# Gate weights for all experts in one GpSimd product, their sum and the row places on ScalarE

## The reference

```python
h = tok_embedding(x)                                  # position, nesting and segment tables times W
h = h + attn(layernorm(h))                            # 8 heads, kernelised attention in chunks of 128
h = h + ffn(layernorm(h))

def ffn(x):                                           # the part that the change touches
    gates = softmax(x @ Wg + bg)
    vals, idx = top_k(gates, 2)
    vals = vals / (sum(vals) + 0.01)
    w = sum(one_hot(idx, 8) * vals)                   # weight of each expert for each token, 0 for six of them
    y = relu(x @ W1[e] + b1[e]) @ W2[e] + b2[e]       # for each expert e
    return sum over e of w[e] * y[e]
```

## Time and profile before

| | |
|---|---|
| median of the runs | 360.71 us |
| profiled execution | 361.17 us |
| its span, first to last instruction | 359.4 us |
| mean granted TensorE clock | 0.981 |
| TensorE busy | 336.3 us, 94% |
| VectorE busy | 309.7 us, 86% |
| ScalarE busy | 251.1 us, 70% |
| GpSimd busy | 210.9 us, 59% |

### The profile page before, as it was taken

The page is one execution under the profiler, slowest core; times in us unless marked ns, Lnnn a source line. Parts: engine busy times, 40 slices in busy tenths (PEclk is TensorE's granted clock), DMA queues, the critical chain, the costliest instruction groups (busy, mean ns, idle before and its releaser), DMA issues.

```text
span 359.4 us, 11506 instructions
## 1 busy us (share of the span) xinstructions
PE 336.3 (94%) x3017; PEld 293.4 (82%) x3017; DVE 309.7 (86%) x1214; ACT 251.1 (70%) x665; POOL 210.9 (59%) x413
## 2 busy tenths in 40 slices
PE   7959999999999999999998799999999999999982
PEld 2525788888878887878886699999999999999982
DVE  6778899999988999999999687998997777678986
ACT  1644878988877987877976477676776677667730
POOL 7010311677777677777776877887875455545520
PEclk9985999999999999999999999999999999999998
DMA  6066660000110001000010312232333322226859
GB/s 165 19 181 168 208 219 3 11 25 35 36 36 25 12 35 34 33 25 17 24 35 34 86 44 80 81 89 87 106 112 90 88 76 64 78 80 190 247 143 275
DMA packets 33131, 30.46 MB, mean 85 GB/s; under 512 B 4701, under 2 KB 27320, under 8 KB 33080
## 3 DMA queue, kind: packets, MB, share of 16 engines
q1 hardware_dynamic: 25848, 18.81, 18.5%
q0 software_dynamic: 4224, 9.18, 7.6%
q10 hardware_dynamic: 3008, 1.89, 1.8%
HBM read 16.42 MB, written 13.44 MB: 83 GB/s over the span
## 4 chain that ended last, share of the span: by engine, by line
PE 80%; DVE 8%; issue 4%; DMA 2%; ACT 2%; SPq 1%; POOL 0%; DVEq 0%; ACTq 0%; POOLq 0%
PE ps_oy L1826 9%; PE ps_vc L1826 9%; PE ps_out L1816 8%; PE ps_out L1719 8%; PE ps_oy L1736 7%; PE ps_q L1816 7%; PE ps_vc L1709 5%; PE ps_qT L1701 3%; PE ps_oy L1729 3%; PE ps_k L1667 2%; PE ps_qT L1808 2%; PE ps_k L1816 2%; PE ps_vc L1690 2%; PE ps_vc L1692 2%; PE ps_vc L1691 2%
## 5 line engine op out<-in xcount | busy, mean ns | idle before, releaser
L773 POOL DMA_INDIRECT y_dram<-heads_out,place x68 | 68.8, 1011 | 46.5 <-ACT heads_out L950 36.8
L750 POOL DMA_INDIRECT slots_dram<-rows,row_id x64 | 64.5, 1007 | 18.4 <-issue 17.6
L941 ACT ACTIVATE k_prime<-ps_out,b_T 128x128 f32<-128x128 f32 x105 | 31.0, 365 | 19.3 <-PE ps_out L1816 18.6
L941 ACT ACTIVATE k_prime<-ps_q,b_T 128x128 f32<-128x128 f32 x108 | 31.7, 365 | 17.2 <-PE ps_q L1816 17.0
L1826 PE MATMUL ps_oy<-w_tile,k_prime 128*128 128x128 f32 x288 | 38.6, 277 | 1.2 <-issue 1.2
L1826 PE MATMUL ps_vc<-w_tile,k_prime 128*128 128x128 f32 x280 | 37.4, 277 | 0.8 <-issue 0.6
L1816 PE MATMUL ps_out<-sT,w_tile 128*128 128x128 f32 x280 | 37.0, 275 | 0.0
L1719 PE MATMUL ps_out<-context,qT 128*128 128x130 f32 x256 | 36.9, 288 | 0.0
L1826 PEld LDWEIGHTS ps_oy<-w_tile,k_prime 128*128 128x128 f32 x288 | 35.0, 192 | 2.0 <-issue 1.9
L715 POOL TENSOR_TENSOR rstd<-moments,ln_eps 128x4 f32<-128x4 f32 (+1 forms) x19 | 3.8, 199 | 55.3 <-DVE moments L1062 53.5
L1469 DVE COPY w_tile<-w_all 128x640 f32 x71 | 35.6, 502 | 0.1
(11 more groups left out here) (293 smaller groups left out, 894.6 us busy)
## 6 DMA issues: line engine op xcount, KB each, us to landing
qkv_rows<-slots_dram SPq DMA_DIRECT2D x71, 72.0 KB
y_sum<-y_dram SPq DMA_DIRECT2D x14, 256.0 KB, 3.5
w_all<-in_L_ffn_W SPq DMA_DIRECT2D x1, 2048.0 KB, 13.7
w_all<-in_L_ffn_W SPq DMA_DIRECT2D x8, 256.0 KB, 4.5
out<-h SPq DMA_DIRECT2D x6, 256.0 KB, 5.1
y_dram<-heads_out,place POOLq DMA_INDIRECT x68
y_dram<-y_sum SPq DMA_DIRECT2D x2, 512.0 KB, 4.6
slots_dram<-rows,row_id POOLq DMA_INDIRECT x64, 2.3
```

What stands on the lines that cost most here:

```text
L750: nc.gpsimd.indirect_dma_start(slots_dram[:, :], bass.IndirectOffsetOnAxis(row_id[:, place_of(p, a), j, k:k + 1], 0), rows[:, place_of(p, ...
L773: nc.gpsimd.indirect_dma_start(y_dram[:, :], bass.IndirectOffsetOnAxis(place[:, a, :], 0), y[:, a, :], None).then_inc(s_placed[a], 16)
L941: last = nc.scalar.activation(hT[:, a % 2, c, :], ps_up[a % 2][0][:, c * P:c * P + P], ACT.Relu, bias=b1_T[:, bass.ds(experts[0] * FC + c, ...
```

## The change

The rows now carry weights of all eight experts, not only of the two chosen ones: all exponentials times one factor. So no weights have to be picked by the choices.

- VectorE's `below_top` takes the largest logit from the unsorted `logits`, and writes second less largest into `below_second` (one instruction more). `choose` waits for the places of the sequence before and no longer for its weights.
- ScalarE's `exps_of` makes one exponential per tile with a sum over the eight experts (`accum_out`), and one more of `below_second`: three ACTIVATEs for one. A new `row_places`, right behind it, waits for the mask and writes the places of both tiles into `rows`: two ACTIVATEs with the token number as bias.
- GpSimd's `weigh` shrinks from fourteen instructions with two waits on other engines to five with one. `scatter` now waits for places and weights too.
- `weigh_last` on VectorE loses three of its eight instructions.

```diff
@@ weigh (GpSimd)
                 pool.wait_ge(s_exps, p + 1)
-                step.done(nc.gpsimd.tensor_tensor(partial[:, :, :], exps[:, :, :], denom_by[:, :, :], ALU.mult))
-                width = E // 2
-                while width:
-                    step.done(nc.gpsimd.tensor_tensor(partial[:, :, 0:width], partial[:, :, 0:width],
-                                                      partial[:, :, width:2 * width], ALU.add))
-                    width //= 2
-                step.done(nc.gpsimd.tensor_tensor(weight[:, :, 0], partial[:, :, 0], minus_one[:, :], ALU.pow))
-
-                pool.wait_ge(s_mask, p + 1)
-                step.add(nc.gpsimd.tensor_tensor(second_at[:, :, :], chosen[:, :, 1, :],
-                                                 second[:, None, :].to_broadcast([P, 2, E]), ALU.mult))
-                step.done(nc.gpsimd.tensor_tensor(weight[:, :, 1], weight[:, :, 0], exps[:, :, 1], ALU.mult))
-                nc.gpsimd.tensor_tensor(rows[:, place_of(p, a), :, D + E:ROW], second_at[:, :, :],
-                                        token_id[:, span(2 * p, 2), None].to_broadcast([P, 2, E]), ALU.add)
-                step.done(nc.gpsimd.tensor_tensor(chosen_w[:, :, :, :], chosen[:, :, :, :],
-                                                  weight[:, :, :, None].to_broadcast([P, 2, TOP, E]), ALU.mult))
-                nc.gpsimd.tensor_tensor(rows[:, place_of(p, a), :, D:D + E], chosen_w[:, :, 0, :], chosen_w[:, :, 1, :],
-                                        ALU.add).then_inc(s_weighed, 1)
+                step.add(nc.gpsimd.tensor_tensor(partial[:, :], exps_sum[:, :], top_eps[:, :], ALU.mult))
+                step.done(nc.gpsimd.tensor_tensor(top_two[:, :], exp_second[:, :], one[:, :], ALU.add))
+                step.done(nc.gpsimd.tensor_tensor(partial[:, :], partial[:, :], top_two[:, :], ALU.add))
+                step.done(nc.gpsimd.tensor_tensor(weight[:, :], partial[:, :], minus_one[:, :], ALU.pow))
+                nc.gpsimd.tensor_tensor(rows[:, place_of(p, a), :, D:D + E], exps[:, :, :],
+                                        weight[:, :, None].to_broadcast([P, 2, E]), ALU.mult).then_inc(s_weighed, 1)
@@ scatter (GpSimd)
                 pool.wait_ge(s_id, p + 1)
+                if not (isinstance(p, int) and p in LAST):
+                    pool.wait_ge(s_row_at, p + 1)
+                    pool.wait_ge(s_weighed, p + 1)
@@ exps_of and row_places (ScalarE)
                 act.wait_ge(s_below, p + 1)
                 weighed(act, p - 1)
-                nc.scalar.activation(exps[:, :, :], below[:, :, :], ACT.Exp).then_inc(s_exps, 1)
+                for k in range(2):
+                    nc.scalar.activation(exps[:, k, :], below[:, k, :], ACT.Exp, accum_out=exps_sum[:, k:k + 1])
+                nc.scalar.activation(exp_second[:, :], below_second[:, :], ACT.Exp).then_inc(s_exps, 1)
+
+            def row_places(p, a):
+                act.wait_ge(s_mask, p + 1)
+                for k in range(2):
+                    last = nc.scalar.activation(rows[:, place_of(p, a), k, D + E:ROW], chosen[:, k, 1, :], ACT.Identity,
+                                                bias=token_id[:, span(2 * p + k, 1)], scale=float(B * S))
+                last.then_inc(s_row_at, 1)
@@ sequence (ScalarE)
                     if j == 0 and live(p - 3):
                         exps_of(p - 3)
+                        row_places(p - 3, 1 - a)
@@ after the sequences (ScalarE)
             exps_of(SEQS - 3)
+            row_places(SEQS - 3, 1)
             act.wait_ge(s_b1, 1)
@@ below_top and choose (VectorE)
-                nc.vector.tensor_tensor(below[:, :, :], top[:, :, :], top[:, :, 0:1].to_broadcast([P, 2, E]),
+                nc.vector.tensor_tensor(below_second[:, :], top[:, :, 1], top[:, :, 0], ALU.subtract)
+                nc.vector.tensor_tensor(below[:, :, :], logits[:, :, :], top[:, :, 0:1].to_broadcast([P, 2, E]),
                                         ALU.subtract).then_inc(s_below, 1)
-                weighed(dve, p - 1)
+                if isinstance(p, int) and p - 1 in LAST:
+                    dve.wait_ge(s_last_weighed, p - LAST[0])
+                else:
+                    wait(dve, s_row_at, p)
@@ weigh_last (VectorE)
-                step.done(nc.vector.tensor_reduce(last_denom[:, :], exps[:, :, :], AX.X, ALU.add))
-                step.done(nc.vector.scalar_tensor_tensor(last_denom[:, :], last_denom[:, :], TOP_EPS, exps[:, :, 1],
+                step.done(nc.vector.scalar_tensor_tensor(last_denom[:, :], exps_sum[:, :], TOP_EPS, exp_second[:, :],
                                                          ALU.mult, ALU.add))
-                step.done(nc.vector.tensor_tensor(last_weight[:, :, 1], last_weight[:, :, 0], exps[:, :, 1], ALU.mult))
-                step.done(nc.vector.tensor_tensor(last_chosen_w[:, :, :, :], chosen[:, :, :, :],
-                                                  last_weight[:, :, :, None].to_broadcast([P, 2, TOP, E]), ALU.mult))
-                nc.vector.tensor_tensor(rows[:, place_of(p, a), :, D:D + E], last_chosen_w[:, :, 0, :], last_chosen_w[:, :, 1, :],
-                                        ALU.add).then_inc(s_last_weighed, 1)
+                nc.vector.tensor_tensor(rows[:, place_of(p, a), :, D:D + E], exps[:, :, :],
+                                        last_weight[:, :, None].to_broadcast([P, 2, E]), ALU.mult).then_inc(s_last_weighed, 1)
```

More of the change, by code:

```diff
@@ L222, in lm_tower_kernel @@
         minus_one = sb("minus_one", [P, 2])
-        second = sb("second", [P, E])
         table_id = sb("table_id", [TR, 1])
@@ L302, in lm_tower_kernel @@
         top = sb("top", [P, 2, E])
+        below_second = sb("below_second", [P, 2])
+        exps_sum = sb("exps_sum", [P, 2])
+        exp_second = sb("exp_second", [P, 2])
+        top_eps = sb("top_eps", [P, 2])
+        one = sb("one", [P, 2])
         top_id = sb("top_id", [P, 2, E], u32)
@@ L310, in lm_tower_kernel @@
         last_denom = sb("last_denom", [P, 2])
[L311 to L316, removed]
+        last_weight = sb("last_weight", [P, 2])
+        partial = sb("partial", [P, 2])
+        top_two = sb("top_two", [P, 2])
+        weight = sb("weight", [P, 2])
         next_row = sb("next_row", [P, E])
@@ L453, in lm_tower_kernel @@
         s_id = sem("row_ids_ready")
+        s_row_at = sem("row_places_ready")
         s_weighed, s_last_weighed = sem("weights_ready"), sem("last_weights_ready")
@@ L651, in _ @@
             nc.gpsimd.memset(minus_one[:, :], -1.0)
-            nc.gpsimd.memset(second[:, :], float(B * S))
-            nc.gpsimd.memset(denom_by[:, :, 0:TOP], 1.0 + TOP_EPS)
-            nc.gpsimd.memset(denom_by[:, :, TOP:E], TOP_EPS)
+            nc.gpsimd.memset(top_eps[:, :], TOP_EPS)
+            nc.gpsimd.memset(one[:, :], 1.0)
             for j in range(2):
@@ L757, in sequence @@
                     weigh(p - 3, 1 - a)
-                    pool.wait_ge(s_weighed, p - 2)
                     scatter(p - 3, 1 - a)
@@ L762, in sequence @@
                 scale(p, a)
-            sequences(pool, step, sequence, 24)
+            sequences(pool, step, sequence, 16)
             def place_y(n, a, i, experts):
@@ L780, in _ @@
             weigh(q, q % 2)
-            pool.wait_ge(s_weighed, q + 1)
             scatter(q, q % 2)
@@ L1253, in weigh_last @@
                 dve.wait_ge(s_exps, p + 1)
-                step.done(nc.vector.tensor_reduce(last_denom[:, :], exps[:, :, :], AX.X, ALU.add))
-                step.done(nc.vector.scalar_tensor_tensor(last_denom[:, :], last_denom[:, :], TOP_EPS, exps[:, :, 1],
+                step.done(nc.vector.scalar_tensor_tensor(last_denom[:, :], exps_sum[:, :], TOP_EPS, exp_second[:, :],
                                                          ALU.mult, ALU.add))
                 step.done(nc.vector.tensor_scalar(last_denom[:, :], last_denom[:, :], 1.0, None, ALU.add))
-                step.done(nc.vector.reciprocal(last_weight[:, :, 0], last_denom[:, :]))
-                step.done(nc.vector.tensor_tensor(last_weight[:, :, 1], last_weight[:, :, 0], exps[:, :, 1], ALU.mult))
+                step.done(nc.vector.reciprocal(last_weight[:, :], last_denom[:, :]))
                 nc.vector.scalar_tensor_tensor(rows[:, place_of(p, a), :, D + E:ROW], chosen[:, :, 1, :], float(B * S),
```

1 line of the change is left out of this document (removed).

## The result

| | before | after |
|---|---|---|
| median of the runs beside each other | 360.81 us (4 runs) | 367.73 us (4 runs, 367.17 to 368.33) |
| profiled execution, its span | 361.17, 359.4 us | 367.69, 365.9 us |
| TensorE busy | 336.3 us, 94% | 341.0 us, 93% |
| VectorE busy | 309.7 us, 86% | 308.9 us, 84% |
| ScalarE busy | 251.1 us, 70% | 261.1 us, 71% |

The changed kernel takes 1.0167 times the time of the one before (95% interval 1.0097 to 1.0236). The forecast was 367.0 us, slower. GpSimd lost 15.5 us of work, ScalarE gained 10, and the whole got 6.5 us longer.

A forecast was written before the change was run, and what follows sets the result against it. A ring of ScalarE and TensorE was taken to bound the attention stage; 2.31 + 1.97 + 1.05 + 1.15 - 0.2 = +6.3 us on 360.71 gave 367.0 us, with ends 363.9 and 371.9 and a range of 363.0 to 371.0.

The forecast's parts named there:

- The ring: Attention sequence: ScalarE's part 5.74 us, hand-over 0.21, TensorE's part 4.57 make the 10.52 us period; after, T = 10.17 + d.
- The slack: Inside the ring: 0.24 us of ScalarE's wait for the shift and 0.11 of hand-over; only d below 0.35 is hidden.
- The delay d: How much later `oT_copy` starts on ScalarE behind the exponentials and places: 0.94 us taken, 0.69 low, 1.34 high.
- the low end: Third exponential ends after 0.45 us, places start at 0.53 behind the mask; d 0.69 us, period 10.86, total +3.2.
- Four written-out periods: Attention stage, p = 3 to 7: four periods of 11.11 us for 42.13 together, +2.31 us (+1.31 to +3.91).
- Six periods of the loop: Attention stage, p = 8 to 14: six periods of 11.11 us for 64.69 together, +1.97 us (+0.47 to +4.37).
- p = 14 and 15: p = 14: 0, VectorE is late there; p = 15: `k_exp` stands behind the late mask and two places, +1.05 us.
- End of the stage: `row_places(13)` waits for its mask between `exps_of(13)` and the b1 copy: +1.15 us (1.0 to 1.6).
- VectorE and GpSimd: VectorE: -0.2 us from the shorter `weigh_last`; GpSimd: nine instructions less, some 1.35 us of `weigh`, worth 0.
- Hidden: Rival: ScalarE's 1.24 us idle in each sequence takes the added work, 360.7 us; decided at d = 0.35; chance 0.06.
- Faster, by GpSimd: Rival: shorter `weigh` ends ScalarE's waits for the shift, 357.2 us; needs d below 0.35 and late GpSimd; chance 0.10.
- Slower still: Rival: sums are separate instructions at full cost and each place waits out the one before, above 371 us; chance 0.03.

The follow-up runs named there:

- e3: The kernel before with nine useless ScalarE copies of 128x2 added right behind `exps_of`; 365.43 us, ratio 1.0105.
- e4b: The kernel before with nine useless ScalarE copies behind `qT_copy` of the odd tile, ahead of ScalarE's 1.24 us wait; 360.67 us, ratio 0.9980.
- e4: The kernel before with nine useless ScalarE copies in the second half of the sequence, behind `q_exp` of the odd tile; 370.75 us, ratio 1.0256.
- e1: The changed kernel with the places made by GpSimd as before, exponentials and sums left on ScalarE; 360.45 us, ratio 0.9966 to the kernel before.
- e9b: The kernel before given all-expert weights, sums and places on GpSimd, and VectorE's moments made earlier, right behind `choose`; 359.60 us, ratio 0.9921.
- e2: The changed kernel with the sums made by GpSimd, one exponential over 128x16, places left on ScalarE; 367.37 us, ratio 1.0145 to the kernel before.
- e5: The kernel before with GpSimd's `weigh` cut from ten instructions to four, weights unnormalised, nothing added to ScalarE; 361.12 us, ratio 0.9990.
- e7b: The changed kernel with `row_places` moved behind `x2T_copy`, and `row_places(13)` behind the first expert tile; 361.43 us, ratio 1.0003 to the kernel before.
- e11: The changed kernel with both tiles' places made by one VectorE instruction behind the residual; 361.26 us, ratio 0.9973 to the kernel before.

## Why the prediction was right, point by point

The direction, the mechanism and the total held; several terms were off and made up for each other.

*The ring.* Right that ScalarE and TensorE release each other in a ring in which the exponentials stand and the idle 1.24 us don't (e3, e4b). Wrong about its ScalarE part, which ends at `x2T_copy`, not at the odd context copy (e4). Any three stretches that follow each other add up to the period; what tells is which of them grows. Before: from the even context copy at 83.17 to the end of `x2T_copy` at 90.06, 6.89 us; 0.15 to the embedding at 90.21; 3.48 to the next context copy at 93.69; together 10.52. After: 7.38, 0.15 and 3.48, together 11.01. With these ends only ScalarE's part grew, by 0.49 us. With the forecast's ends all three change: 5.74, 0.21 and 4.57 became 6.22, 0.10 and 4.69.

*The slack.* The forecast found 0.35 us of it: 0.24 of the wait for the shift and 0.11 of the hand-over. The hand-over gives nothing: behind the odd context copy it does fall from 0.21 to 0.10, as forecast, but TensorE then stands before the embedding, 0.15 us behind `x2T_copy` as before. The wait gives 0.37, more than the 0.24 listed: with it `normalize_second` started 0.24 us behind the end of `qT_copy`, without it 0.13 us ahead of that end (88.22 against 87.75 + 0.60). 0.88 - 0.37 = 0.51, within 0.02 of the growth. So 0.35 was good by luck, two errors that cancel; e1's hidden d of 0.38 confirms it from the side. And the wait is not the only floor: e9b, without it and with a d of 0.10, stays at 10.51 to 10.53 in most periods, TensorE's own work. Either floor hides a d of some 0.38 (10.51 - 10.13).

*The delay d.* 0.88 us measured for 0.94 taken. The sums are instructions of their own, as feared, but start only 0.10 us after what they follow; the third exponential starts 0.39 us behind the first and ends after 0.58 us, for 0.72 taken. The places start 0.59 us behind the exponential, at the mask (0.53 was the earliest forecast), and the pair with what follows takes 0.51 (0.44 taken). The forecast's middle value let the end of the exponentials decide; the mask does, as in the low end's reasoning (e2). An earlier start and longer places cancel, so the size of d is in part luck.

*Four written-out periods.* +2.19 for +2.31. Three are 11.00, the fourth 11.32, since the mask comes late in p = 6.

*Six periods of the loop.* +2.86 for +1.97: this term was mis-sized, by 0.9 us. The mask's 0.47 us behind the exponential was read in p = 5 and used for all sequences. In the loop it ends later, and the trace of before had it. There, in p = 10, the exponential on ScalarE and the mask on VectorE:

```profile
138.86 0.20 ACT L897 ACTIVATE exps<-below 128x16 f32<-128x16 f32 x1
```
```profile
139.86 0.16 DVE L1136 TENSOR_TENSOR mask<-chosen 128x16 bf16<-128x16 f32 x1
```

The mask ends 1.16 us behind the exponential there; in the six sequences p = 8 to 13 of the kernel before it is 0.59 to 1.16, after 0.67 to 0.80. Besides, the places start 0.03 us behind the mask in p = 5 but 0.15 behind it in the loop:

```profile
142.37 0.16 DVE L1141 TENSOR_TENSOR mask<-chosen 128x16 bf16<-128x16 f32 x1
```
```profile
142.68 0.49 ACT L894 ACTIVATE rows<-chosen,token_id 128x8 f32<-128x8 f32 x2 [0.38 <-DVE mask L1141]
```

With 0.67 to 0.80 + 0.15 + 0.51 - 0.22 the delay is 1.11 to 1.24 us, and 10.13 + d gives 11.24 to 11.37, the periods that the loop has (11.21 to 11.37).

*p = 14 and 15.* +1.06 for 0 + 1.05. The places start at once behind the late mask (200.01 to 200.04), and `k_exp` stands 1.04 us behind its end, for 1.00 forecast. Cut at the exponentials, 0.47 of this falls in p = 14, and 0.59 in p = 15; but the mask, on which `k_exp` now hangs, stands only 0.13 us later behind the `exps_of` of p = 14 than it did (13.18 for 13.05).

*End of the stage.* +1.08 for +1.15. The mask ends 0.77 us behind the exponential (0.76 forecast), and TensorE passes the delay on whole: its wait grew by 1.09 us.

*VectorE and GpSimd.* The stretch behind the b1 copy is 0.13 us shorter for 0.2. That agrees by luck: the fall of the clock there, 2.04 us by the seventh tile, wasn't forecast, and the expert stage made it up. GpSimd's `weigh` went from ten instructions to five in the trace, not from fourteen to five, so five less and not nine; the relief of 1.38 us (3.07 to 1.69 in p = 5) is the 1.35 of the forecast. e5 shows that GpSimd's relief is worth nothing measurable by itself.

*Not forecast.* The setup is 0.57 us shorter. Over all kernels run here the first exponential starts between 62.0 and 63.6 us; whether the change has a part in it was not tried.

*The rivals.* "Hidden" named the right point: a d of 0.37 to 0.38 is covered, as e1, e7b and e11 show; the change went beyond it by the places and their wait alone. "Faster, by GpSimd" fails on its second condition (e5), not only on d. "Slower still" needed the sums at full length and the places one behind the other; neither happened.

## What to carry to other kernels

An engine's idle time in a busy table is room only at the place where it lies: follow the ring of two in-order engines until both hand-overs close, and ask of new work whether it stands inside. An instruction put into an in-order queue with a wait costs the wait to all that follows it, however small it is; the same places of the rows cost nothing measurable when GpSimd, VectorE or a later point of ScalarE's own queue made them. And read the offset that decides, here the mask behind the exponential, in each sequence and not in one.

## What the runs showed of the hardware

A sum over columns by `accum_out` is a ScalarE instruction of its own, with its own record. The groups by line and shape:

```profile
L888 ACT ACTIVATE exps<-below 128x8 f32<-128x8 f32 x32 | 6.2, 195 | 2.7 <-DVE below L1127 2.7
L888 ACT ACTIVATION_READ_ACCUMULATOR exps<-below 128x1 f32 x32 | 6.0, 188 | 0.0
```

Each lasts about 190 ns, but the next starts 0.09 to 0.10 us after its start; nine copies of 128x2 take 0.93 us. So these small instructions without a wait cost half of what their mean duration says, while the wait at `normalize_second` took away an overlap of 0.13 us beside its idle time. And the wait for the mask ended 0.03 to 0.04 us behind the end of the mask in the written-out sequences, 0.13 to 0.15 in the hardware loop; what makes that difference was not tried.
